# Two pieces of expert 1's third weight matrix split behind that expert's row pieces instead of ahead of them

## What is computed

```python
buf = jnp.zeros((E, cap, D), x.dtype).at[e_s, pos].set(xn[t_s], mode='drop')
gu = jnp.einsum('ecd,efd->ecf', buf, W12)
g, u = (gu[..., :D_FF], gu[..., D_FF:])
h = jax.nn.silu(g) * u
y = jnp.einsum('ecf,edf->ecd', h, W3)
y_slot = y[e_s, jnp.minimum(pos, cap - 1)] * (w_s * kept.astype(x.dtype))[:, None]
out = jnp.zeros((T, D), x.dtype).at[t_s].add(y_slot)
```

## Time and profile before

| what | value |
|---|---|
| time, median of 3 runs | 542.4 us (542.34 to 545.05) |
| the profiled execution: its time | 546.42 us |
| its span, from the first to the last instruction | 544.5 us |
| mean granted TensorE clock, share of full speed | 0.955 |
| PE busy | 488.8 us, 90% of the span |
| DVE, ACT, POOL busy | 364.9, 299.0, 208.6 us |
| expert stage | from about 230 us to the end |

### The profile page before, as it was taken

One profiled execution on the slowest core, in us unless ns is written; L12 is line 12 of the kernel. 1 busy time (PEld: TensorE's weight loads), 2 busy tenths in 40 slices (PEclk: granted clock), 3 DMA queues, 4 the chain that ended last, 5 costly groups with the idle time before them and its releaser, 6 DMA issues.

```text
span 544.5 us, 10727 instructions
## 1 busy us (share of the span) xinstructions
PE 488.8 (90%) x3529; PEld 452.5 (83%) x3551; DVE 364.9 (67%) x854; ACT 299.0 (55%) x757; POOL 208.6 (38%) x272
## 2 busy tenths in 40 slices
PE   5799999999999887289699899999999999999991
PEld 4588887777777766289599799999999999999991
DVE  6757878889998997547658285376753767644340
ACT  3679878687777753417546273274732646433140
POOL 8535776777878556500020303203031030301212
PEclk9899999899999987779799899999999999999996
DMA  8858422314142611162456536146460555101011
GB/s 265 223 98 261 78 40 71 68 60 79 41 78 58 206 48 51 49 225 108 164 138 205 129 88 175 16 132 186 127 183 10 136 174 138 21 11 19 11 20 19
DMA packets 41649, 57.33 MB, mean 105 GB/s; under 512 B 3721, under 2 KB 38576, under 8 KB 39552
## 3 DMA queue, kind: packets, MB, share of 16 engines
q1 hardware_dynamic: 35168, 48.62, 30.8%
q0 software_dynamic: 6144, 8.07, 8.9%
q10 hardware_dynamic: 288, 0.00, 0.0%
HBM read 36.24 MB, written 16.72 MB: 97 GB/s over the span
## 4 chain that ended last, share of the span: by engine, by line
PE 54%; DVE 1%; DMA 1%; issue 1%; ACT 1%; POOL 1%; POOLq 0%; DVEq 0%
PE bank L1438 17%; PE bank L1439 16%; PE bank L1440 16%; PE bank L1361 2%; PE bank L1432 2%; DMA stage<-in_w3T 1%; ACT wh L714 0%; POOL expert_rows L484 0%; DMA expert_rows<-xr,slotu 0%; PE bank L1304 0%; DVE bXl L1099 0%; POOL out_tokens L546 0%; DVE wl L1092 0%; PE bank L1238 0%; DVE ysc L1142 0%
## 5 line engine op out<-in xcount | busy, mean ns | idle before, releaser
L546 POOL DMA_INDIRECT out_tokens<-ysc,rows x32 | 49.4, 1542 | 254.8 <-DVE ysc L1142 248.3
L1438 PE MATMUL bank<-bXh,wh 128*128 128x384 f32 (+1 forms) x384 | 122.7, 320 | 2.7 <-issue 2.5
L1439 PE MATMUL bank<-bXl,wh 128*128 128x384 f32 (+1 forms) x384 | 122.5, 319 | 0.0
L1440 PE MATMUL bank<-bXh,wl 128*128 128x384 f32 (+1 forms) x384 | 122.4, 319 | 0.0
L749 ACT ACTIVATE sil<-bank 128x384 f32<-128x384 f32 (+1 forms) x96 | 43.7, 456 | 133.1 <-PE bank L1440 133.0
L1121 DVE TENSOR_TENSOR hF<-sil,bank 128x384 f32<-128x384 f32 (+1 forms) x96 | 48.9, 510 | 81.0 <-ACT sil L749 81.0
L633 ACT ACTIVATE p<-bank,nm 128x128 f32<-128x128 f32 x256 | 73.6, 386 | 16.7 <-DVE nm L924 16.7
L1438 PEld LDWEIGHTS bank<-bXh,wh 128*128 128x128 f32 x384 | 73.1, 190 | 3.1 <-issue 3.1
L1438 PE MATMUL bank<-wh,hH 128*128 128x256 f32 x256 | 74.4, 291 | 0.3 <-DVE ysc L1142 0.3
L1440 PEld LDWEIGHTS bank<-bXh,wl 128*128 128x128 f32 x384 | 73.2, 191 | 0.0
L1439 PEld LDWEIGHTS bank<-bXl,wh 128*128 128x128 f32 x384 | 73.1, 190 | 0.0
(11 more groups left out here) (146 smaller groups left out, 884.0 us busy)
## 6 DMA issues: line engine op xcount, KB each, us to landing
stage<-in_w12T SPq DMA_DIRECT2D x16, 1024.0 KB, 4.9
stage<-in_w3T SPq DMA_DIRECT2D x8, 1024.0 KB, 5.6
expert_rows<-padrow SPq DMA_DIRECT2D x8, 662.5 KB, 7.6
rows<-expert_rows SPq DMA_DIRECT2D x7, 662.5 KB, 4.2
kM<-k SPq DMA_DIRECT2D x64, 64.0 KB, 2.4
cT<-in_ctxT SPq DMA_DIRECT2D x8, 256.0 KB, 3.2
out_tokens<-x_all SPq DMA_DIRECT2D x8, 256.0 KB, 2.3
x_all<-in_x SPq DMA_DIRECT2D x2, 640.0 KB, 8.5
```

The source lines that it names most:

```text
L546: pool.indirect_dma_start(out=out, out_offset=bass.IndirectOffsetOnAxis(rows[par][:, c, D + E:ROW].bitcast(U32), 0), in_=ysc[par][:, c, :] ...
L1438: nc.tensor.matmul(out_ap, ah, bh, start=start, stop=False)
L1439: nc.tensor.matmul(out_ap, ah, bl, start=False, stop=False)
L1440: return nc.tensor.matmul(out_ap, al, bh, start=False, stop=stop)
```

## The change

For expert 0 alone, the border between the two batches moves from piece 10 to piece 8, on ACT and on DVE. Pieces 8 and 9 of expert 1, the first half of its w3, are split behind the four row groups, together with pieces 10 and 11, not ahead of them. No instruction is added or taken out, and the streams of PE, POOL and SP are what they were.

```diff
@@ ACT, expert() @@
                 if not last:
-                    for k in range(FT - 5 if first else FT, FT + 2 if first else PIECES):
+                    for k in range(FT - 5 if first else FT, FT if first else PIECES):
                         high(i + par, 1 - par, k)
                     for a in range(4):
                         rows_high(e + 1, 1 - par, a)
                     if first:
-                        for k in range(FT + 2, PIECES):
+                        for k in range(FT, PIECES):
                             high(i + par, 1 - par, k)
```

## The result

| | time, median of 4 runs | profiled execution | its span |
|---|---|---|---|
| before | 543.15 us (542.34 to 545.05) | 546.42 us | 544.5 us |
| changed | 536.12 us (534.19 to 536.22) | 534.19 us | 532.3 us |

The changed kernel takes 0.9862 of the time before, 95% interval 0.9834 to 0.989: 6.0 to 9.0 us less. Of before a run more was taken beside the changed kernel, so its median here is 543.15 and not 542.4.

What follows compares the result with a forecast made beforehand. The prediction took PE as the bound, with a 5.2 us wait for DVE's row split. It summed 5.4 us of earlier start and 1.2 us of clock to 6.7 us: 542.4 to 535.7 us, range 533.5 to 538.5.

Runs made afterwards that it cites:

- pad22: Changed kernel with 22 idle transposes on PE ahead of its wait for the scatter, where it rests anyway: 532.11 us, ratio 0.9819 against before.
- unroll_pe: Changed kernel with PE's loop over experts 2 to 5 written out, other engines keeping their loops: 534.53 us, ratio 0.9859 against before.
- border7: Changed kernel with one piece more, piece 7, behind the row groups on ACT and DVE: 538.37 us, ratio 0.9883 against before.
- half_load: Kernel before, order kept, with w3 of expert 1 loaded as two transfers of 512 KB: 540.73 us against 543.33, ratio 0.9951.
- dve_part: Kernel before with the change made on DVE alone, ACT keeping its old order: 542.84 us against 543.98, ratio 0.9978.
- border9: Kernel before with the border moved to piece 9, one piece in place of two, on both engines: 542.10 us against 543.98, ratio 0.9956.

## What to carry to other kernels

An engine that works strictly in order turns one early need for a late load into a wait for all that stands behind it; look for work whose inputs are ready and whose result another engine waits for, and let it pass, on every engine of the chain at once. Look for what comes due next before moving more: one piece further gained 0.4 us at the place and lost 1.5 us behind it, and 1.6 us more by the clock. Where a wait has no releaser and stands at a taken branch, try a few idle instructions ahead of it in a place where the engine rests anyway; pad22 has the lowest median of all runs (532.11 us), though its interval overlaps that of the changed kernel, so that it is faster is shown in its trace (next 26.41 and not 29.0) and not by that comparison. Timed on the same chip, unroll_pe, which keeps the wait, has 534.53.

## What the runs showed of the hardware that I had not expected

- A shift of PE's code by 44, 88 or 132 instructions, with the same work behind it, moves waits of 1.7 to 3.0 us between three branches, or removes them all. The medians go from 532.1 to 542.0 us; the waits in the traces account for about 6 us of that, a low clock behind each for some more.
- A rest of 2.6 us cost nothing in clock in the changed kernel, and a rest of 2.5 us in before was followed by 3.4 us at 1.2 GHz. It is no accident of one trace: the same rest, 2.4 to 2.7 us long, cost nothing in four traces of the changed order and about 1.5 us in five in which PE had waited 2.9 to 5.2 us for the row split some 35 us earlier, and as much in border7, where it had waited 1.16 us for a hidden tile. What links the two is not shown. A rest of 2.87 us in half_load cost 1.55 us of low clock.
- A transfer of 512 KB landed in 3.4 us, with a second one of 512 KB issued 0.4 us behind it, where 1 MB took 5.3 to 5.75 us in before, dve_part and border9: half the size took about 2 us off.
